# One-hot operands laid out contiguously, and a root product issued in pieces, in a graph network kernel

## The chip, the cores and the metric

The kernel runs on one NeuronCore of a Trainium2 chip. The metric is the device time of one execution in microseconds (us). The engines are TensorE (PE; its weight loads are listed as PEld), VectorE (DVE), ScalarE (ACT), GpSimd (POOL) and SyncE (SP, which here issues DMAs).

## The reference

A stack of graph convolutions over 625 nodes with 768 features and 10625 edges. The first layer is relational, with 34 edge types:

```python
h = relu(layernorm(x))                       # 625 x 768
seg = edge_type * n + dst                    # 34 * 625 segments
agg = segment_sum(h[src], seg)
cnt = segment_sum(ones, seg)
mean = agg / maximum(cnt, 1)
h1 = einsum('rni,rio->no', mean, W_rel) + h @ W_root + b_rgcn
...                                          # then four GCN and three RGCN layers, 3 edge types
```

The edges (src, dst, edge_type) are inputs and are known only on the device, so the kernel sorts them there.

## The kernel before

**Preparation** (`prepare`, the first 248 us) sorts the edges by type into *slots*: 186 tiles of 128 slots, three tiles to a *unit*, each unit of one edge type. Sorting is done with one-hot matrices and matmuls. The edges lie as 125 partitions x 85 columns.

- *Ranks.* VectorE makes `is_key` (edge type one-hot), TensorE sums it per column (`ps_tile`), over partitions (`lower`) and over columns (`offsets`, `bases`), into six PSUM banks. VectorE multiplies and adds these up to one position for each edge (`place`), and from it `slot_of` and `tile_of`.
- *Slots.* In five chunks of 17 columns VectorE makes `is_slot` (17 x 128), `is_tile` (17 x 186) and two products `at_slot` (source and destination number in the slot). For each column TensorE runs two matmuls (`slots(n)`): weights `at_slot[:, n % 2, i, :, c]`, streamed operand `is_tile[:, n % 2, :, c]`. The column number `c` is the innermost dimension of both, so one column's elements are 17 elements (34 bytes) apart. One chunk is 34 matmuls. Buffers are double: chunk n waits for `chunk_used` of n-2.
- *Counts.* `is_node` (128 slots x 125 nodes, six groups of 31 tiles) are the weights of 186 matmuls with five streamed columns (`counts(n)`), which give the number of edges of each node in each unit.
- *Inversion.* After ranks of the nodes within a unit, ten steps (`is_rank_of(i)` on VectorE, `invert(i)` with 31 matmuls on TensorE; 128 weight columns, 31 elements apart, nine streamed columns) give each unit's list of target nodes, `row_list`.
- *Root product.* `h @ W_root + b` in fp32, ten outputs of 125 x 384 (`root(n)`), each a bias matmul and six matmuls. The profile counts each of these fp32 matmuls twice (x12 for six). The ten calls stand at chosen places between the steps above. ScalarE copies each out (`take(n)`), and SyncE stores two of them at a time to DRAM (`sums`), as 125 rows.

Then all engines meet at a barrier.

**Means** (`add_means`, 248 to 998 us) loops over about 34 units: gather 384 rows, select and sum them with `pick` matmuls, multiply with the unit's 768 x 768 weights (loaded each unit, fp32 split in two parts), scatter-add to `sums`. `pick` is made from `slot_dst` and the unit's target list `list_now`, read back from the DRAM tensor `targets`. *Beside* the units the same sort is done for the later layers with their 3 edge types: units 0 to 3 make places on VectorE; in the next five units VectorE makes `is_tile` (2 x 120 x 17) and `is_slot` (128 x 17) and TensorE runs `columns(n)` behind the unit's products: 17 matmuls of 240 streamed columns, again with `c` innermost. The order of work on every engine is the order of the code. A second pass repeats `columns` once behind the last unit for keys with many edges. The layers follow (998 to 1912 us); nothing in them is touched.

## Time and profile before

| | |
|---|---|
| time, three runs | median 1918.2 us (1913.0 to 1918.44) |
| the profiled execution | 1914.25 us, its span 1912.6 us |
| PE busy, PEld busy | 1792.1 us (94%), 1594.5 us (83%) |
| DVE, ACT, POOL busy | 956.0 (50%), 632.5 (33%), 314.7 (16%) |
| granted TensorE clock, mean | 0.928 |

Busy time is the time in which an engine has an instruction in work; a busy TensorE need not run at its peak. The span is from the first to the last instruction of the profiled execution; its own time is 1.65 us more. A granted clock of 1.00 is 2.4 GHz, and 0.50 is 1.2 GHz.

### The profile page before, as it was taken

How to read it: one execution, taken by the hardware profiler on the slowest of the kernel's cores; microseconds unless marked ns; L12 is line 12 of the kernel's file. 1: busy time of each engine (PE TensorE's matmuls, PEld its weight loads, DVE VectorE, ACT ScalarE, POOL GpSimd, SP SyncE). 2: the span in 40 equal slices, each digit the busy share in tenths (PEclk: the TensorE clock that was granted, in tenths of full speed). 3: DMA queues.
4: the chain of work that ended last, by engine and by line, in shares of the span. 5: the costliest groups of instructions: out<-in, count | busy, mean ns of one | idle time of the engine just before them, and what ended most of it. 6: DMA issues, size and time to landing. Idle time of an engine off the chain costs nothing. (4 is left out here: it accounts for less than half of the span.)

```text
span 1912.6 us, 28877 instructions
## 1 busy us (share of the span) xinstructions
PE 1792.1 (94%) x10081; PEld 1594.5 (83%) x10082; DVE 956.0 (50%) x1439; ACT 632.5 (33%) x853; POOL 314.7 (16%) x277
## 2 busy tenths in 40 slices
PE   5999969999999999999958897999999999899988
PEld 2458668777899999898848897999988999899988
DVE  6313559756667766765445556223333333433363
ACT  3200045534555555565422223122112222222220
POOL 0000036353334444444220000000000000000000
PEclk9765789999999999999978998999998999999999
DMA  3210058655879878998533121222112222132111
GB/s 119 93 36 0 19 168 227 187 160 162 231 201 266 233 213 238 267 283 248 152 67 107 58 64 45 55 69 84 39 33 75 75 74 63 34 96 59 38 50 48
DMA packets 96001, 226.47 MB, mean 118 GB/s; under 512 B 10274, under 2 KB 36116, under 8 KB 95940
## 3 DMA queue, kind: packets, MB, share of 16 engines
q1 hardware_dynamic: 72951, 153.22, 25.4%
q0 software_dynamic: 19104, 70.00, 15.8%
q10 hardware_dynamic: 3885, 2.41, 0.4%
q8 instruction: 42, 0.69, 0.2%
q14 instruction: 19, 0.16, 0.0%
HBM read 186.23 MB, written 39.36 MB: 118 GB/s over the span
## 5 line engine op out<-in xcount | busy, mean ns | idle before, releaser
L521 PE MATMUL layers_ps_o<-layers_w_hi,layers_g_hi 128*125 128x384 f32 (+1 forms) x1040 | 360.8, 347 | 4.2 <-DVE layers_w_lo L387 4.2
L522 PE MATMUL layers_ps_o<-layers_w_lo,layers_g_hi 128*125 128x384 f32 (+1 forms) x1040 | 360.4, 347 | 0.0
L523 PE MATMUL layers_ps_o<-layers_w_hi,layers_g_lo 128*125 128x384 f32 (+1 forms) x1040 | 359.9, 346 | 0.0
L1955 PE MATMUL l_means_ps<-l_means_w_hi,l_means_g_hi 128*128 128x512 f32 (+1 forms) x912 | 239.6, 344 | 7.1 <-DVE l_means_g_lo L1813 7.1
L1955 PE MATMUL l_means_ps<-l_means_w_hi,l_means_g_lo 128*128 128x512 f32 (+1 forms) x912 | 236.4, 340 | 0.0
L1955 PE MATMUL l_means_ps<-l_means_w_lo,l_means_g_hi 128*128 128x512 f32 (+1 forms) x912 | 235.4, 340 | 0.0
L1602 ACT CAST l_means_w_hi<-w_raw 128x768 fp32r<-128x768 f32 x204 | 170.3, 838 | 196.3 <-PE l_means_ps L1955 184.8
L1802 DVE TENSOR_TENSOR l_means_w_lo<-w_raw,l_means_w_hi 128x768 fp32r<-128x768 f32 x204 | 187.0, 949 | 75.4 <-ACT l_means_w_hi L1602 57.9
L548 PE MATMUL layers_ps_g<-a,h_hi 125*128 125x316 f32 x840 | 197.1, 317 | 28.4 <-DVE h_lo L158 12.2
L521 PEld LDWEIGHTS layers_ps_o<-layers_w_hi,layers_g_hi 128*125 128x125 f32 x1040 | 193.8, 186 | 11.2 <-issue 5.9
L523 PEld LDWEIGHTS layers_ps_o<-layers_w_hi,layers_g_lo 128*125 128x125 f32 x1040 | 193.7, 186 | 5.3
L522 PEld LDWEIGHTS layers_ps_o<-layers_w_lo,layers_g_hi 128*125 128x125 f32 x1040 | 193.6, 186 | 5.2
L548 PE MATMUL layers_ps_g<-a,h_lo 125*128 125x316 f32 x840 | 196.1, 316 | 0.0
L1939 PE MATMUL l_means_ps<-l_means_pick,l_means_e_hi 128*128 128x256 f32 (+1 forms) x612 | 171.6, 309 | 15.9 <-DVE l_means_e_lo L1797 15.2
L1955 PEld LDWEIGHTS l_means_ps<-l_means_w_hi,l_means_g_hi 128*128 128x128 f32 x912 | 153.4, 190 | 26.6 <-DVE l_means_w_lo L1802 4.2
L324 ACT CAST layers_w_hi<-layers_w_raw 128x768 fp32r<-128x768 f32 (+1 forms) x104 | 89.9, 865 | 256.9 <-PE layers_ps_o L523 247.6
L1955 PEld LDWEIGHTS l_means_ps<-l_means_w_lo,l_means_g_hi 128*128 128x128 f32 x912 | 154.7, 190 | 20.8
L1955 PEld LDWEIGHTS l_means_ps<-l_means_w_hi,l_means_g_lo 128*128 128x128 f32 x912 | 154.8, 189 | 19.7
L406 DVE SCALAR_TENSOR_TENSOR h_rows<-layers_ps_o,layers_inv_rows,h_rows 125x768 f32<-125x768 f32 (+1 forms) x45 | 47.8, 1062 | 247.0 <-PE layers_ps_o L523 246.9
L548 PEld LDWEIGHTS layers_ps_g<-a,h_hi 125*128 125x128 f32 x840 | 146.0, 196 | 30.0 <-DVE h_lo L158 12.7
L1939 PE MATMUL l_means_ps<-l_means_pick,l_means_e_lo 128*128 128x256 f32 (+1 forms) x612 | 168.8, 305 | 0.7 <-issue 0.7
L1534 POOL DMA_INDIRECT sums<-l_means_y,l_means_row_now x76 | 130.3, 1714 | 204.5 <-ACT l_means_y L1637 180.9
(305 smaller groups left out, 2234.5 us busy)
## 6 DMA issues: line engine op xcount, KB each, us to landing
w_raw<-in_L_gnn_W_rel SPq DMA_DIRECT2D x204, 384.0 KB, 7.4
layers_w_raw<-in_L_gnn_w_rel SPq DMA_DIRECT2D x39, 384.0 KB, 3.3
layers_w_raw<-in_L_gnn_w_rel SPq DMA_DIRECT2D x21, 448.0 KB, 4.1
layers_a_raw<-adj SPq DMA_DIRECT2D x9, 769.0 KB
layers_w_raw<-in_L_gnn_W SPq DMA_DIRECT2D x18, 384.0 KB, 5.4
l_means_list_now<-targets SPq DMA_DIRECT2D x34, 192.0 KB
layers_w_raw<-in_L_gnn_w_root SPq DMA_DIRECT2D x13, 384.0 KB, 3.9
layers_w_raw<-in_L_gnn_w_root SPq DMA_DIRECT2D x7, 448.0 KB, 6.2
```

Source lines behind the costliest of these rows:

```text
L324: nc.scalar.copy(w_hi[:, f, :], w_raw[:, f % ring, :]).then_inc(w_hi_ready, 1)
L406: v.scalar_tensor_tensor(to, ps, by, base, ALU.mult, ALU.add).then_inc(o_taken, 1)
L521: t.matmul(out, g_hi[:, f, rows], w_hi[:, f, cols], start=(f == 0), stop=False)
L522: t.matmul(out, g_hi[:, f, rows], w_lo[:, f, cols], start=False, stop=False)
L523: mm = t.matmul(out, g_lo[:, f, rows], w_hi[:, f, cols], start=False, stop=(f == fc - 1))
L548: mm = t.matmul(ps_g[:, buf, at:at + PART[p]], rows[:, k, f * 128:(f + 1) * 128], a[:, k, cols], start=(k == 0 and part == 0), stop=(k == ...
L1534: nc.gpsimd.indirect_dma_start(out=sums, in_=y[:, j, :], in_offset=None, compute_op=ALU.add, out_offset=bass.IndirectOffsetOnAxis(ap=row_n ...
L1602: nc.scalar.copy(w_hi[:, f, :], w_raw[:, f, :]).then_inc(w_hi_ready, 1)
L1802: v.tensor_tensor(w_lo[:, f, :], w_raw[:, f, :], w_hi[:, f, :].bitcast(F32), ALU.subtract)\
L1939: mm = t.matmul(sums, e[:, j, f * 128:(f + 1) * 128], pick[:, j, 0:cols], start=(j == 0 and part == 0), stop=(j == UNIT - 1 and part == 1))
L1955: mm = t.matmul(ps_y[j][:, o0:o1], g[:, f, at], w[:, f, o0:o1], start=(f == 0 and opens and g is g_hi and w is w_hi), stop=(f == fc - 1 an ...
```

## The change

1. The one-hot operands of `slots` and `columns` have the slot or tile number innermost and the column outside. VectorE's comparisons take their second operand in short repeated runs (`SLOT_RUN` 8, `TILE_RUN` 6, `KEY_RUN` 5): `slot_of`, `tile_of`, `loads_by`, `values` and `tile_sums` are stored 5 to 8 times over. The expanded counters `slot_iota` and `tile_iota`, which ScalarE made, are gone.
2. `is_node` has 128 columns for each tile in place of 125.
3. The root product goes in pieces of one matmul (60 in all): four behind each chunk of slots, one behind each group of counts, ten behind the turned counts, one behind each of eight inversion steps, the rest at the end. The bias is split in two fp32r rows.
4. The statistics and scales of the layer norm stand before the places on VectorE, and the transposes of `h` before the first slots on TensorE. The sum that gives `lots` goes ahead of the rank matmuls.
5. Each half of a root tile is stored alone, as 112 and 13 rows.
6. The first unit's target list is made by a matmul on the chip (`ps_first`); the lists are stored to `targets` in the next block.

```diff
-        at_slot = slot_flat[0:EP].rearrange("p (b i s c) -> p b i s c", b=2, i=2, c=chunk)
-        is_tile = tile_flat[0:EP].rearrange("p (b t c) -> p b t c", b=2, c=chunk)
+        at_slot = slot_flat[0:EP].rearrange("p (b i c s) -> p b i c s", b=2, i=2, c=chunk)
+        is_tile = tile_flat[0:EP].rearrange("p (b c t) -> p b c t", b=2, c=chunk)
...
-                then(v.tensor_tensor(is_slot[:], slot_iota[:], slot_of[:, at].unsqueeze(1).broadcast_to([EP, SLOT, chunk]),
-                                     ALU.is_equal))
+                then(v.tensor_tensor(in_runs(is_slot[:], SLOT_RUN),
+                                     by_runs(iota[0:EP, 0:SLOT], SLOT_RUN).unsqueeze(1).broadcast_to(slot_rows),
+                                     slot_of[:, at].unsqueeze(2).broadcast_to(slot_rows), ALU.is_equal))
...
-                                node_of[:, n * group:(n + 1) * group].unsqueeze(1).broadcast_to([SLOT, NP, group]),
+                                node_of[:, n * group:(n + 1) * group].unsqueeze(1).broadcast_to([SLOT, SLOT, group]),
...
-                t.matmul(out, ones_f[:, 0:NP], bias_row[:, cols], start=True, stop=False)
-                for f in range(fc):
+            def root(count):
+                for i in range(done[0], done[0] + count):
+                    n, f = i // fc, i % fc
...
+                        t.matmul(out, one_row[:, 0:NP], bias_hi[:, cols], start=True, stop=False)
+                        t.matmul(out, one_row[:, 0:NP], bias_lo[:, cols], start=False, stop=False)
                     mm = t.matmul(out, root_g[:, f, n // 2 * NP:(n // 2 + 1) * NP], root_w[:, f, cols],
                                   start=False, stop=(f == fc - 1))
...
-                        mm = t.matmul(ps_slot[:, i, 0:tiles], at_slot[:, n % 2, i, :, c], is_tile[:, n % 2, :, c],
+                        mm = t.matmul(ps_slot[:, i, 0:tiles], at_slot[:, n % 2, i, c, :], is_tile[:, n % 2, c, :],
...
+            for n in range(EC // chunk):
+                slots(n)
+                root(4)
+            for n in range(tiles // group):
+                counts(n)
+                root(1)
...
             for i in range(2 * NT):
                 invert(i)
-                if i == 4:
-                    root(7)
+                root(1 if i < 8 else 0)
...
+            t.matmul(ps_first, ones[:], first_list[:].rearrange("p t s -> p (t s)"), start=True, stop=True)\
+                .then_inc(first_spread, 1)
+            root(2)
+            root(10 * fc - done[0])
...
-            for to, count_to, times in ((slot_iota, SLOT, COLUMNS), (tile_iota, tiles2, COLUMNS), (node_iotas, NP, LOTS)):
...
-                    mm = t.matmul(ps_b[:, 0:2 * tiles2], is_slot[:, :, c], is_tile[:, :, :, c],
+                    mm = t.matmul(ps_b[:, 0:2 * tiles2], is_slot[:, c, :], is_tile[:, c, :, :],
```

On TensorE between the first slots and the third chunk, before (`prep_ps<-prep_is_tile,prep_at_slot` are the slots, `prep_root_w,prep_root_g` the root product, `h_rows` the transposes):

```order
L1139 MATMUL prep_ps<-ident,h_rows 128x125 x4
L1160 MATMUL prep_ps<-prep_is_tile,prep_at_slot 128x186 [waits prep_chunk_ready]
L1160 MATMUL prep_ps<-prep_is_tile,prep_at_slot 128x186 x33
L1150 MATMUL prep_ps<-prep_bias_row,prep_ones_f 125x384 [waits prep_root_g_ready,prep_root_loaded]
L1152 MATMUL prep_ps<-prep_root_w,prep_root_g 125x384 x6
L1160 MATMUL prep_ps<-prep_is_tile,prep_at_slot 128x186 [waits prep_chunk_ready]
L1160 MATMUL prep_ps<-prep_is_tile,prep_at_slot 128x186 x33
L1150 MATMUL prep_ps<-prep_bias_row,prep_ones_f 125x384
L1152 MATMUL prep_ps<-prep_root_w,prep_root_g 125x384 x6
L1150 MATMUL prep_ps<-prep_bias_row,prep_ones_f 125x384 [waits prep_o_taken]
L1152 MATMUL prep_ps<-prep_root_w,prep_root_g 125x384 x6
```

and now:

```order
L1178 MATMUL prep_ps<-ident,h_rows 128x125 x4
L1209 MATMUL prep_ps<-prep_is_tile,prep_at_slot 128x186 [waits prep_chunk_ready]
L1209 MATMUL prep_ps<-prep_is_tile,prep_at_slot 128x186 x33
L1197 MATMUL prep_ps<-prep_bias_hi,prep_one_row 125x384 [waits prep_one_row_ready,prep_root_g_ready,prep_bias_ready,prep_root_loaded]
L1198 MATMUL prep_ps<-prep_bias_lo,prep_one_row 125x384
L1199 MATMUL prep_ps<-prep_root_w,prep_root_g 125x384 x4
L1209 MATMUL prep_ps<-prep_is_tile,prep_at_slot 128x186 [waits prep_chunk_ready]
L1209 MATMUL prep_ps<-prep_is_tile,prep_at_slot 128x186 x33
L1199 MATMUL prep_ps<-prep_root_w,prep_root_g 125x384 x2
L1197 MATMUL prep_ps<-prep_bias_hi,prep_one_row 125x384
L1198 MATMUL prep_ps<-prep_bias_lo,prep_one_row 125x384
L1199 MATMUL prep_ps<-prep_root_w,prep_root_g 125x384 x2
```

The transposes of `h_rows` moved ahead of all slots; the root product's two whole outputs and more became four matmuls behind each chunk.

On TensorE behind the last slots, before (rows of 128 x 5 and 125 x 5 are the counts):

```order
L1160 MATMUL prep_ps<-prep_is_tile,prep_at_slot 128x186 x33
L1170 MATMUL prep_ps<-prep_is_tile,prep_at_slot 125x5 [waits prep_nodes_ready]
L1170 MATMUL prep_ps<-prep_is_tile,prep_at_slot 125x5 x30
L1170 MATMUL prep_ps<-prep_is_tile,prep_at_slot 125x5 [waits prep_nodes_ready]
L1170 MATMUL prep_ps<-prep_is_tile,prep_at_slot 125x5 x30
L1150 MATMUL prep_ps<-prep_bias_row,prep_ones_f 125x384 [waits prep_o_taken]
L1152 MATMUL prep_ps<-prep_root_w,prep_root_g 125x384 x6
L1170 MATMUL prep_ps<-prep_is_tile,prep_at_slot 125x5 [waits prep_nodes_ready]
L1170 MATMUL prep_ps<-prep_is_tile,prep_at_slot 125x5 x30
```

and now:

```order
L1209 MATMUL prep_ps<-prep_is_tile,prep_at_slot 128x186 x33
L1199 MATMUL prep_ps<-prep_root_w,prep_root_g 125x384 x2
L1197 MATMUL prep_ps<-prep_bias_hi,prep_one_row 125x384 [waits prep_o_taken]
L1198 MATMUL prep_ps<-prep_bias_lo,prep_one_row 125x384
L1199 MATMUL prep_ps<-prep_root_w,prep_root_g 125x384 x2
L1219 MATMUL prep_ps<-prep_is_tile,prep_at_slot 128x5 [waits prep_nodes_ready]
L1219 MATMUL prep_ps<-prep_is_tile,prep_at_slot 128x5 x30
L1199 MATMUL prep_ps<-prep_root_w,prep_root_g 125x384
L1219 MATMUL prep_ps<-prep_is_tile,prep_at_slot 128x5 [waits prep_nodes_ready]
L1219 MATMUL prep_ps<-prep_is_tile,prep_at_slot 128x5 x30
L1199 MATMUL prep_ps<-prep_root_w,prep_root_g 125x384
```

The counts have 128 rows of output, and a root matmul stands behind each group of 31.

On VectorE from the tile numbers on, before (L1005 to L1010 are the first chunk's one-hots, L88 the statistics; the places are made ahead of these rows):

```order
L997 CAST prep_tile_of<-prep_tile_i 125x85 [waits prep_step]
L1005 TENSOR_TENSOR prep_is_slot<-prep_slot_iota,prep_slot_of 125x2176 [waits prep_iotas_ready,prep_step]
L1007 TENSOR_TENSOR prep_is_tile<-prep_tile_iota,prep_tile_of 125x3162 [waits prep_step]
L1010 TENSOR_TENSOR prep_at_slot<-prep_is_slot,prep_loads 125x2176 x2
L1013 ISA [waits prep_step]
L1017 TENSOR_SCALAR prep_type_row<-prep_ps 62x62 [waits prep_types_summed]
L1018 TENSOR_SCALAR prep_type_col<-prep_ps 62x1 [waits prep_step]
L1019 CAST s_plan<-prep_type_row 1x62 [waits prep_step]
L1020 TENSOR_SCALAR prep_same_type<-prep_type_row,prep_type_col 62x62
L88 BN_STATS prep_stats<-x_rows 125x6 [waits prep_x_loaded1]
L88 BN_STATS prep_stats<-x_rows 125x6
```

and now, behind the statistics and ahead of the tile numbers (L1015 makes the places):

```order
L97 BN_AGGR prep_moments<-prep_stats 125x2 x4
L99 TENSOR_SCALAR prep_var<-prep_moments 125x5 [waits prep_step]
L100 RECIPROCAL prep_rstd<-prep_var 125x5 [waits prep_step]
L78 TENSOR_TENSOR prep_tmp<-prep_rstd 125x5 [waits prep_rooted]
L79 TENSOR_TENSOR prep_tmp<-prep_tmp,prep_var 125x5 [waits prep_step]
L80 TENSOR_SCALAR prep_tmp<-prep_tmp 125x5 [waits prep_step]
L81 TENSOR_TENSOR prep_rstd<-prep_rstd,prep_tmp 125x5 [waits prep_step]
L1003 SCALAR_TENSOR_TENSOR prep_shift<-prep_moments,prep_rstd 125x5 [waits prep_step]
L1005 TENSOR_TENSOR prep_bias_lo<-prep_at_slot,prep_bias_hi 1x768 [waits prep_bias_hi_ready]
L1015 TENSOR_TENSOR prep_early<-prep_ps,prep_early 125x1530 [waits prep_ranked]
L1015 TENSOR_TENSOR prep_early<-prep_ps,prep_early 125x1020 [waits prep_ranked,prep_step]
L1015 TENSOR_TENSOR prep_early<-prep_ps,prep_early 125x340 [waits prep_ranked,prep_step]
```

The scales and the low part of the bias, and the statistics ahead of them, moved from behind the first chunk to before the places.

## Rows read from the trace of the kernel before

**Rows 1.** Windows view: busy time, granted clock (PEclk), DMA share by stage.
```profile
core 0: us, PE busy (x) PEld busy (x) DVE busy (x) ACT busy (x) POOL busy (x), PEclk, DMA share, GB/s
35.00:127.00 92.00, 91.56 (x256) 42.28 (x256) 29.41 (x41) 19.86 (x32) 0.00 (x0) 0.75 0.17 55
127.00:180.00 53.00, 48.37 (x202) 44.03 (x200) 15.54 (x16) 0.48 (x1) 4.10 (x3) 0.56 0.08 23
180.00:247.00 67.00, 56.52 (x404) 38.15 (x404) 34.66 (x46) 3.24 (x8) 0.00 (x0) 0.73 0.06 19
247.00:975.00 728.00, 710.81 (x4166) 622.32 (x4167) 483.70 (x812) 379.34 (x540) 303.26 (x247) 0.96 0.76 214
```

**Rows 2.** Timeline, TensorE: start, duration, op, shape, count; slots, then root products.
```profile
71.53 11.65 PE L1160 MATMUL prep_ps<-prep_is_tile,prep_at_slot 125*128 125x186 f16 x34
...
84.67 6.97 PE L1152 MATMUL prep_ps<-prep_root_w,prep_root_g 128*125 128x384 f32 x12
...
92.41 4.13 PE L1152 MATMUL prep_ps<-prep_root_w,prep_root_g 128*125 128x384 f32 x12
```

**Rows 3.** Timeline, VectorE, one-hots of a chunk; idle before and its releaser in brackets.
```profile
83.21 1.36 DVE L1005 TENSOR_TENSOR prep_is_slot<-prep_slot_iota,prep_slot_of 125x2176 f16<-125x2176 f16 x1 [13.61 <-PE prep_ps L1160]
84.61 1.90 DVE L1007 TENSOR_TENSOR prep_is_tile<-prep_tile_iota,prep_tile_of 125x3162 f16<-125x3162 f16 x1
...
127.54 0.35 DVE L1030 TENSOR_SCALAR s_src_index<-prep_ps 128x186 int32<-128x186 f32 x1 [38.49 <-PE prep_ps L1160]
```

**Rows 4.** Timeline, VectorE, the start of the program.
```profile
17.98 0.15 DVE L969 COPY prep_ends<-prep_ps 34x1 f32<-34x1 f32 x1 [5.05 <-PE prep_ps L1201]
...
20.94 3.56 DVE L986 TENSOR_TENSOR prep_early<-prep_ps,prep_early 125x1530 f32<-125x1530 f32 x3 [0.93 <-PE prep_ps L1205]
24.53 4.05 DVE L991 TENSOR_TENSOR prep_early<-prep_early 125x1445 f32<-125x1445 f32 x6
...
35.96 3.76 DVE L88 BATCH_NORM_STATS2 prep_stats<-x_rows 125x6 f32<-125x384 f32 x8
```

**Rows 5.** Timeline, TensorE and VectorE, counts and inversion.
```profile
153.49 26.82 PE L1170 MATMUL prep_ps<-prep_is_tile,prep_at_slot 128*125 128x5 f16 x124
...
180.35 0.48 DVE L1049 TENSOR_SCALAR prep_present<-prep_ps 125x310 f16<-125x310 f32 x1 [11.19 <-PE prep_ps L1170]
...
197.42 3.85 PE L1179 MATMUL prep_ps<-prep_tile_iota,prep_early 125*128 125x9 f16 x62
...
217.53 6.75 DVE L1064 TENSOR_TENSOR prep_early<-prep_early,prep_rank_lo 125x3968 f16<-125x3968 f16 x3 [6.91 <-PE prep_ps L1179]
```

**Rows 6.** Timeline, the means loop and its second pass: VectorE, SyncE, TensorE.
```profile
374.42 0.56 DVE L1813 TENSOR_TENSOR l_means_g_lo<-l_means_ps,l_means_g_hi 128x384 fp32r<-128x384 f32 x1 [9.13 <-ACT l_means_g_hi L1616]
...
465.04 0.34 SPq L1477 DMA_DIRECT2D l_means_list_now<-targets  x1
...
491.29 0.34 SPq L1477 DMA_DIRECT2D l_means_list_now<-targets  x1
...
509.36 0.34 SPq L1477 DMA_DIRECT2D l_means_list_now<-targets  x1
...
979.23 7.56 PE L1903 MATMUL l_means_ps<-e_raw,l_means_again_slot 125*128 125x240 f16 x17 [3.63 <-DVE e_raw L1768]
```

**Rows 7.** Timeline and source line L1911, TensorE: contiguous f16 columns (ns min/median/max).
```profile
496.94 0.71 PE L1911 MATMUL l_means_ps<-l_means_is_dst,l_means_is_src 128*125 128x315 f16 x4
...
L1911 PE MATMUL l_means_ps<-l_means_is_dst,l_means_is_src x124: 295/298/507, 496.9 to 992.4; 128*125 128x315 f16 x124
```

**Rows 8.** Timeline, VectorE, one-hots in runs of four.
```profile
990.16 0.42 DVE L1782 TENSOR_TENSOR l_means_is_src<-l_means_node_iotas,l_means_slot_src 128x500 f16<-128x500 f16 x1 [2.83 <-issue]
```

**Rows 9.** Timeline, three waits: fifth unit, last store, first selection.
```profile
350.35 1.01 PE L1955 MATMUL l_means_ps<-l_means_w_hi,l_means_g_hi 128*128 128x512 f32 x2 [2.88 <-DVE l_means_g_lo L1813]
...
240.99 0.26 SPq L833 DMA_DIRECT2D sums<-h_rows  x1
...
251.84 1.08 DVE L1791 TENSOR_SCALAR l_means_pick<-l_means_list_now,s_slot_dst 128x384 fp32r<-128x384 f32 x3 [20.55 <-DMA l_means_list_now<-targets]
```

More of the change, by code:

```diff
@@ L976, in _ @@
             v.tensor_scalar(behind[:], iota[0:types, 0:units], ends[:, 0:1], None, ALU.is_ge).then_inc(behind_ready, 1)
+            for k in range(1, NT):
+                ins = statistics(k)
+            then(ins)
+            row_scales(v, then, dve, inverted, rooted, 1, moments, stats, var, rstd, tmp, range(NT))
+            v.scalar_tensor_tensor(shift[:], moments[:, :, 0], -1.0, rstd[:], ALU.mult, ALU.mult).then_inc(scales_ready, 1)
+            dve.wait_ge(bias_hi_ready, 1)
+            v.tensor_tensor(bias_lo[:], bias_raw, bias_hi[:].bitcast(F32), ALU.subtract).then_inc(bias_ready, 1)
             for b0, b1 in ((0, 3), (3, rank_banks - 1), (rank_banks - 1, rank_banks)):
@@ L1188, in _ @@
             mm.then_inc(tiles_summed, 1)
+            pe.wait_ge(sums_copied, 1)
+            t.matmul(ps_total, tile_sums[:, :, 0], ones[0:EC, 0:2], start=True, stop=True, skip_group_check=True)\
+                .then_inc(totalled, 1)
             for b in range(rank_banks):
@@ L1202, in _ @@
                 .then_inc(lots_summed, 1)
+            pe.wait_ge(offsets_ready, 1)
+            for b in range(rank_banks):
+                t.matmul(ranks(b), ones[0:EC, 0:EP], offsets[:, keys_of(b), :].rearrange("p k c -> p (k c)"),
+                         start=False, stop=False, skip_group_check=True)
             pe.wait_ge(bases_ready, 1)
@@ L1210, in _ @@
                 .then_inc(types_summed, 1)
-            slots(0)
+            pe.wait_ge(placed, 1)
             for f in range(fc):
                 turn(f)
-            slots(1)
-            root(0)
-            slots(2)
-            root(1)
-            root(2)
-            slots(3)
-            root(3)
-            slots(4)
-            counts(0)
-            counts(1)
-            root(4)
-            for n in range(2, tiles // group):
+            for n in range(EC // chunk):
+                slots(n)
+                root(4)
+            for n in range(tiles // group):
                 counts(n)
+                root(1)
             pe.wait_ge(present_ready, 1)
@@ L1277, with add_means @@
 Background = namedtuple("Background", "src dst etype kinds adj adj_all ident h node_types emb")
-def add_means(nc, tag, units, w_rel, rows, sums, plan, src_index, slot_dst, row_index, row_inv, targets, e_raw, w_raw, second):
+def add_means(nc, tag, units, w_rel, rows, sums, plan, src_index, slot_dst, row_index, row_inv, targets, list_rows, list_now,
+              e_raw, w_raw, second):
     width = rows.shape[1]
```

252 lines of the change are left out of this document (142 added, 110 removed).

## The prediction

> **What bounds the kernel now.** I read the windows by stage first. From 35 to 247 us TensorE is busy for nearly all of the time, but its granted clock is 0.75, 0.56 and 0.73, against 0.96 in the means loop, and VectorE is busy for less than half [rows 1]. So preparation is bound by a TensorE that is slow, not short of work. The timeline says what at. A chunk of slots is 34 matmuls of 186 f16 columns in 11.65 us, 343 ns each or 1.84 ns a column [rows 2]. The 315 contiguous f16 columns of L1911 come four in 0.71 us with the last one's 0.30 us in it, so one each 137 ns, 0.43 ns a column [rows 7]. The slots stream elements 34 bytes apart, and VectorE waits for them: 13.6 us before a chunk, 38.5 us before `src_index` [rows 3]. The counts take 26.82 us for 124 matmuls of five columns, 216 ns each; the inversion's, with nine columns, take 3.85 us for 62, 62 ns each [rows 5]. Their weights lie 62 bytes apart alike; 125 columns against 128 is what differs. The means loop is TensorE's too (710.8 of 728 us busy), and the `columns` blocks in it are the slots again: 17 in 7.56 us (the second pass's row; five more of this shape stand in the loop), 445 ns for 240 columns, 1.85 ns a column [rows 1, 6].
>
> **The change part by part.** All against the profiled execution, 1914.25 us.
>
> *Start of chunk 0, later by 3 us.* VectorE's places end at 28.6 us (24.53 + 4.05). Of the waits before them (5.05 and 0.93 us for TensorE, whose strided `offsets` go contiguous and whose `lots` go ahead) I leave 0.5: -5.5. Ahead come the statistics, 3.76 us, some twelve small operations at 0.15 to 0.2, 2.2, and `bias_lo`, 0.95 (768 elements; the adds do 2805 in 4.05 us) [rows 4]. With 0.3 for the runs of five (below) the places end at 30.3. The wider `slot_of` and `tile_of` and the type rows make 2.3, a chunk's one-hots 5.6: ready at 38.1. ScalarE's new copies (`loads_by`, `bias_hi`) stand behind three that it has anyway and end well before; if not, each us late is a us lost.
>
> *One-hots in short runs.* The 2176-element and 3162-element operations take 1.36 and 1.90 us in runs of 17 [rows 3]. Nine cycles of 0.96 GHz for each run of 17 give 1.20 and 1.74, and leave 0.16 us fixed for both; the 500 elements in runs of four take 0.42, which is 0.26 + 0.16 [rows 8]. So runs of 8 and 6 should go at two elements a cycle: 1.29, 1.80, 1.29, 1.29, a chunk 5.6 us. Bound above: one a cycle, 10.7 us. The Trainium skill (Vector Engine (DVE) Microarchitecture Reference, 5.1 Performance modes) says that with two sources a pair may span two rows of odd length, so that odd runs would waste nothing. The rows differ: without the half-filled cycle the fixed parts would be 0.23 and 0.25, and 0.42 for the 500 would be too short. By the page the `offsets` in runs of five (2890 elements) would cost 1.66 us, by the rows 1.97, the 0.3 above; the sum by the page would be 0.3 us less.
>
> *Slots, 127.54 to 68.9.* A matmul of 186 contiguous columns is 81 ns at full clock by 0.43 ns a column (62 ns, the inversion's, bounds it below), 34 are 2.75 us; at half clock 5.5. A root piece is two of the profile's matmuls: 0.69 us at clock 1 (4.13 / 12), 1.16 in the stretch at about half (6.97 / 12) [rows 2]. Bias matmuls appear nowhere in this type; a pair for every six pieces I price as a piece. So slots and four pieces make 6.0 us at full clock and 10.9 at half, against VectorE's 5.6. I take the first at 10, as TensorE comes from idling, and the others at 6.0 (dense, as in the means loop): 38.1 + 10 + 18 + 2.75 = 68.9. **-58.6**.
>
> *Counts, 52.8 to 21.7.* To the first group stays at 4.6 (`is_node` costs 0.05 more); the four pieces behind the last slots lie beside it. Then six steps of 31 x 66 ns = 2.05 and a piece of 0.69 to 1.16, together 2.95, above `is_node`'s 2.3; the last piece is not waited for, 0.3 for handshakes: 4.6 + 17.7 - 0.9 + 0.3. From `src_index` to `present` it is 52.8 us now [rows 3, 5]. **-31.1**.
>
> *From `present` to the last store's issue, 60.6 now* [rows 5, 9]. 34 pieces remain where 30 stood, but seven bias pairs' cheap matmuls replace five fp32 ones, and pieces go between inversion steps where TensorE waits for 2.25 us of `is_rank` [rows 5]. TensorE is busy for 56.5 of 67 us [rows 1], so little is to be had. **0**, from -5 to +4.6 (four pieces at half clock).
>
> *Last store.* One of 375 KB in 125 rows is issued at 240.99 and the block ends near 247; halves of 112 and 13 rows spread otherwise. **-2.5**, from 0 to -3.5.
>
> *First selection.* `pick` waits for a DMA that was issued at the block's start [rows 9]; the list is on the chip now, and ScalarE's `e_hi` is late next. **-2.9**, from 0 to -3.3.
>
> *Columns in five units.* A unit with a block takes 26.25 us (465.04 to 491.29), the next without one 18.07 [rows 6]: 8.2, of which the block itself is 7.56, the rest a slower clock behind it. 17 x 104 ns = 1.8 remain. VectorE's operations lie beside products; it idles 9.13 us at a time there [rows 6], and if this cover went, they would cost 5.2 us a unit. **-32**, from -18 (new block at half clock, slow tail stays) to -33.
>
> *Expanded counters gone from ScalarE.* TensorE waits 2.88 us behind them before the fifth unit [rows 9]; wider `slot_of` and `tile_of` on VectorE give 1 back. **-2**.
>
> *Second pass.* Its block stands alone, from idle: 17 x 0.2 = 3.5 in place of 7.56, and 1.2 more on VectorE ahead. **-3**.
>
> Sum: 58.6 + 31.1 + 2.5 + 2.9 + 32 + 2 + 3 = 132.1, so 1782 for the profiled execution. The median of the runs shown, 1918.2, lies 4 us above it, and runs differ by 5; I say **1784**.
>
> **The rivals.**
> - *TensorE stays at half clock in preparation.* For it: the clock there is 0.56 to 0.75 now [rows 1], weight-bound counts and inversion remain between the pieces, and 84.67 shows seven us of root work that did not lift it [rows 2]. Against it: the root product at 92.41 ran at 1.0. Slots then end at 38.1 + 4 x 10.9 + 5.5 = 87.2, +18; counts +2, the rest +7: 1811. The Trainium skill (TensorE: Matmul & The Clock Gate, HAM oscillation) ties a lasting full clock to bursts without idle gaps; by that the new order, whose gaps are short, would be the forecast's.
> - *One-hots at one element a cycle.* A chunk takes 10.7 us on VectorE; slots end at 32.5 + 53.5 + 2.9 = 88.9, +20; the second pass +4; the loop covers its share: 1808. Against: the runs of four [rows 8].
> - *Contiguous columns stream no faster* (1.84 ns is then something else): chunks end at 38.1 + 4 x (11.65 + 5.4) + 11.65 = 118, 49 us of the slots' gain gone, and all of the 32 and 3: 1868. Against: 0.43 ns [rows 7].
> - *128 node columns load no faster than 125*: six steps of 7.8 us, 29 us lost: 1813.
> - *Slower than before: the short runs cost far more on VectorE.* With p ns an element, chunks alone take 48.5p + 3 us; beyond 1.65 ns the loop's units stretch too (8.3p each, five), and the second pass by 8.3p. That adds 98p - 104 us, and eats the 132 from p = 2.4; at 2.5 it is 1925. The trace's slowest vector row is near 1.4 (4.05 us for 2805 elements).
>
> **How the numbers follow.** Forecast 0.70; half clock 0.12; one element a cycle 0.07; no gain from contiguity 0.05; none from 128 columns 0.04; slower 0.02. The forecast's own range is 1768 to 1802: below, full clock from the first chunk (-4), steps of 2.75 (-1), -5 between `present` and the store, -1 each elsewhere; above, the bounds of its terms but not all at once. The two next cases at 1808 and 1811 are taken in: **1768 to 1815**. A difference of 0.3% (6 us) is about what can be told here. Faster 0.97, same 0.01, slower 0.02.
>
> **What the changed profile would show.** L1209, slots: 34 in 2.8 to 5.5 us; L1219, counts: 31 in about 2.1; L1041 to L1048: 1.29 and 1.80 us; `src_index` near 69, `present` near 91, the last store's issue near 151; units with `columns` 2 us longer than those without; granted clock above 0.9 from 50 to 90 us. The forecast is wrong if the clock falls between pieces, if VectorE's operations are longer than 1.4 us, or if the loop's units turn to another engine or to DMA once the block is short.

## The result and the profile after

The changed kernel takes **1786.0 us** (median of 4 runs, 1783.4 to 1787.1) beside 1915.6 for the kernel before on the same chip (1911.8 to 1918.4): a ratio of **0.932, 95% interval 0.930 to 0.935**. The profiled execution took 1786.46 us, its span is 1784.8 against 1912.6, so 127.8 us are to be accounted for.

The windows view by the stages of [rows 1]; the slots are two rows here, the counts' row is followed by one of four microseconds in it, the last row is the means loop and most of its second pass:

```profile
core 0: us, PE busy (x) PEld busy (x) DVE busy (x) ACT busy (x) POOL busy (x), PEclk, DMA share, GB/s
38.00:50.00 12.00, 12.00 (x82) 9.54 (x82) 11.85 (x9) 3.41 (x1) 0.00 (x0) 0.84 0.19 76
50.00:69.00 19.00, 19.00 (x136) 13.98 (x136) 12.51 (x19) 5.78 (x9) 1.70 (x2) 1.00 0.09 23
69.00:90.00 21.00, 19.67 (x196) 14.66 (x195) 13.23 (x6) 1.21 (x4) 2.45 (x2) 0.59 0.23 74
78.00:82.00 4.00, 4.00 (x48) 3.21 (x47) 2.92 (x2) 0.00 (x0) 0.00 (x0) 0.50 0.00 0
90.00:150.00 60.00, 58.24 (x421) 39.70 (x420) 36.11 (x50) 3.24 (x8) 0.00 (x0) 0.69 0.06 17
154.00:850.00 696.00, 676.80 (x4169) 611.78 (x4169) 486.87 (x813) 377.15 (x540) 293.00 (x247) 0.99 0.79 223
```

Slots have the full clock from 42 us on (1.00 is 2.4 GHz); counts and most of the inversion do not, though TensorE is busy in nearly all of their time.

TensorE's timeline, slots and counts, which answers to [rows 2, 5]:

```profile
37.93 4.82 PE L1209 MATMUL prep_ps<-prep_is_tile,prep_at_slot 125*128 125x186 f16 x34 [5.63 <-DVEq L1051]
...
43.21 2.85 PE L1199 MATMUL prep_ps<-prep_root_w,prep_root_g 128*125 128x384 f32 x8
45.90 2.91 PE L1209 MATMUL prep_ps<-prep_is_tile,prep_at_slot 125*128 125x186 f16 x34
...
70.99 2.04 PE L1219 MATMUL prep_ps<-prep_is_tile,prep_at_slot 128*128 128x5 f16 x31 [1.33 <-DVE prep_at_slot L1075]
72.89 1.62 PE L1199 MATMUL prep_ps<-prep_root_w,prep_root_g 128*125 128x384 f32 x2
74.30 2.00 PE L1219 MATMUL prep_ps<-prep_is_tile,prep_at_slot 128*128 128x5 f16 x31
76.16 1.62 PE L1199 MATMUL prep_ps<-prep_root_w,prep_root_g 128*125 128x384 f32 x2
```

VectorE's timeline, a chunk's one-hots and the ends of slots and counts, which answers to [rows 3, 5]:

```profile
37.86 1.29 DVE L1041 TENSOR_TENSOR prep_is_slot<-prep_iota,prep_slot_of 125x2176 f16<-125x2176 f16 x1
39.18 1.81 DVE L1044 TENSOR_TENSOR prep_is_tile<-prep_iota,prep_tile_of 125x3162 f16<-125x3162 f16 x1
40.91 2.48 DVE L1048 TENSOR_TENSOR prep_at_slot<-prep_is_slot,prep_loads_by 125x2176 f16<-125x2176 f16 x2
...
66.35 0.35 DVE L1062 TENSOR_SCALAR s_src_index<-prep_ps 128x186 int32<-128x186 f32 x1 [5.88 <-PE prep_ps L1209]
...
90.52 0.48 DVE L1081 TENSOR_SCALAR prep_present<-prep_ps 125x310 f16<-125x310 f32 x1 [5.31 <-PE prep_ps L1219]
```

34 slot matmuls take 2.91 us instead of 11.65. A count group takes its 2 us, but the piece behind it lasts from 72.89 to 74.30, 1.42 us, where at the full clock one takes 0.69 (4.13 for twelve of the profile's matmuls, which is six pieces). So each of the counts' and most of the inversion's steps is 3.28 us, and VectorE's 2.29 us of one-hots is not what they go by.

TensorE's timeline at the end of the fifth `columns` block, where the program leaves the loop of five units, closes the lists (L1973) and enters the next loop:

```profile
349.40 1.92 PE L1960 MATMUL l_means_ps<-l_means_cnt 125*128 125x240 f16 x17
...
351.15 0.17 PE L1973 MATMUL l_means_ps<-l_means_zeros 128*128 128x2 f16 x1
355.63 0.38 PE L1996 MATMUL l_means_ps<-l_means_pick,l_means_e_hi 128*128 128x256 f32 x1 [4.31 <-issue]
```

and SyncE's marks of the units around it, which answer to the three of [rows 6]:

```profile
339.54 0.34 SPq L1522 DMA_DIRECT2D list_now<-targets  x1
...
364.32 0.34 SPq L1522 DMA_DIRECT2D list_now<-targets  x1
...
382.38 0.34 SPq L1522 DMA_DIRECT2D list_now<-targets  x1
```

The blocks are down from 7.56 to 1.92 us, yet the last unit with one is 24.78 us long, only 1.5 shorter than before: behind its block TensorE does nothing for 4.31 us, and the releaser is "issue", which means that the profile shows no semaphore that it waited for.

| From and to | forecast | measured |
| --- | --- | --- |
| start to `src_index` | -58.6 | 127.54 to 66.35: -61.2 |
| `src_index` to `present` | -31.1 | 52.81 to 24.17: -28.6 |
| `present` to the last store's issue | 0 | 60.64 to 60.5: -0.1 |
| last store to the means block's first work on ScalarE | -2.5 | 6.75 to 3.1: -3.7 |
| from there to the means' first matmul | -2.9 | 7.92 to 4.98: -2.9 |
| loop: columns and expanded counters | -34 | -30.4 |
| rest of the means and second pass | -3 | -3.9 |
| layers, from their first matmul | 0 | +3.0 |
| sum, us | -132.1 | -127.8 |

The loop's figure is from the first matmul of the means (255.66 and 159.09) to the first unit without a block (509.36 and 382.38). The layers' first matmul is at 1005.07 and 874.24. What the layers' 3 us are is asked of `after_again`.

The first row of the table holds more than the new layout. Before, from 35.33 to 127.5 us, TensorE spent 57.9 us on slot matmuls, 29.0 on four outputs of the root product between them and 5.3 on the transposes of `h`; now, from 37.93 to 66.35, it is 15.8 and 12.4 us (16 pieces and three bias pairs), and the transposes lie in a wait ahead of the first chunk. So the slot matmuls are 42 of the 61.2 us, the root product 17, of which a part is only moved behind the slots, and the transposes 5; the start is 2.6 later. These shares are read from the rows; no run tries the order of the root product by itself.

### The profile page after: what moved, and what is told of

It is laid out like the page before. It is cut to its first block, busy times and chain, and to the rows that moved or that the text cites. A ratio compares the mean times of both kernels' runs of the same rounds, so it can differ in the third digit from the quotient of the medians.

```text
span 1784.8 us, 28899 instructions
## 1 busy us (share of the span) xinstructions
PE 1672.6 (94%) x10082; PEld 1546.7 (87%) x10083; DVE 960.0 (54%) x1444; ACT 626.4 (35%) x852; POOL 303.4 (17%) x276
## 4 chain that ended last, share of the span: by engine, by line
PE 46%; DVE 3%; DMA 1%; ACT 1%; SPq 0%; issue 0%; DVEq 0%
PE layers_ps_g L548 14%; PE layers_ps_o L521 11%; PE layers_ps_o L522 11%; PE layers_ps_o L523 11%; DVE layers_w_lo L387 1%; DMA layers_w_raw<-in_L_gnn_w_root 1%; DMA layers_w_raw<-in_L_gnn_W_gcn 1%; DVE layers_g_lo L392 1%; PE layers_ps_g L572 0%; SPq L127 0%; ACT layers_w_hi L324 0%; DVE h_rows L406 0%; DVE h_lo L456 0%; DVE layers_stats L88 0%; DVE x_rows L406 0%
## 5 line engine op out<-in xcount | busy, mean ns | idle before, releaser
L1996 PE MATMUL l_means_ps<-l_means_pick,l_means_e_hi 128*128 128x256 f32 (+1 forms) x612 | 165.9, 302 | 14.0 <-DVE l_means_e_lo L1854 9.0
L1996 PE MATMUL l_means_ps<-l_means_pick,l_means_e_lo 128*128 128x256 f32 (+1 forms) x612 | 164.7, 299 | 1.9 <-issue 1.9
```

The costliest lines, as they stand in the source:

```text
L1996: mm = t.matmul(sums, e[:, j, f * 128:(f + 1) * 128], pick[:, j, 0:cols], start=(j == 0 and part == 0), stop=(j == UNIT - 1 and part == 1))
```

## The experiments

Theory A: TensorE's price in the slots and columns was the jump of 34 bytes between streamed elements, in the counts the 125 weight columns; what was not gained lies in pieces that ran at 1.2 GHz and in one idle stretch, in which TensorE's program waited for its own next instructions. The rivals: strided weights; the old order's waits; late data behind the columns.

### Which operand's stride it was

```diff
 # tile_strided
-        is_tile = tile_flat[0:EP].rearrange("p (b c t) -> p b c t", b=2, c=chunk)
+        is_tile = tile_flat[0:EP].rearrange("p (b t c) -> p b c t", b=2, c=chunk)
 # weights_strided
-        at_slot = slot_flat[0:EP].rearrange("p (b i c s) -> p b i c s", b=2, i=2, c=chunk)
+        at_slot = slot_flat[0:EP].rearrange("p (b i s c) -> p b i c s", b=2, i=2, c=chunk)
```

> Edit: the changed kernel with only the slots' tile one-hot (the moving operand, 186 columns) laid out as before, element 34 bytes from element; the weights (at_slot) stay contiguous. Theory A (the price of before was the moving operand's stride): the 34 slot matmuls of a chunk take about 11.65 us again instead of 2.91, a chunk some 14.5 instead of 5.75, src_index comes near 110 instead of 66.4 and the time near 1830 us. Rival B (it was the weights' stride): 34 in about 2.9 us and a time within 8 us of the changed kernel's 1786; what is over comes from VectorE, which now writes with a stride (3162 elements, 1.8 us if that costs nothing, 3.3 if it costs the fast mode).

> Edit: the changed kernel with only the slots' weights (at_slot) laid out as before, 34 bytes from element to element; the moving one-hot stays contiguous. Theory A (only the moving operand's stride costs): 34 slot matmuls in about 2.9 us, weight loads near 0.10 us each; VectorE writes two of its four operations of a chunk with a stride, so a chunk lasts 5.75 us if that is free and 7.9 if they fall to one element a cycle, and the time is 1786 to 1797. Rival B (strided weights cost TensorE): 34 matmuls well above 4 us, up to 11.65, and a time up to 1830.

One run each: 1847.7 and 1862.7 us. The timelines of the first chunks, TensorE and VectorE, of `tile_strided`:

```profile
49.53 11.49 PE L1209 MATMUL prep_ps<-prep_is_tile,prep_at_slot 125*128 125x186 f16 x34 [17.33 <-DVEq L1051]
...
66.81 11.50 PE L1209 MATMUL prep_ps<-prep_is_tile,prep_at_slot 125*128 125x186 f16 x34 [0.46 <-DVEq L1051]
...
50.78 13.60 DVE L1044 TENSOR_TENSOR prep_is_tile<-prep_iota,prep_tile_of 125x3162 f16<-125x3162 f16 x1
```

and of `weights_strided`:

```profile
53.94 5.49 PE L1209 MATMUL prep_ps<-prep_is_tile,prep_at_slot 125*128 125x186 f16 x34 [22.30 <-DVEq L1051]
...
56.91 9.42 DVE L1048 TENSOR_TENSOR prep_at_slot<-prep_is_slot,prep_loads_by 125x2176 f16<-125x2176 f16 x1
```

For TensorE theory A holds: with the moving operand alone strided the chunk is back at 11.5 us (338 ns a matmul), with the weights alone 5.49 at a granted clock of 0.50, 161 ns a matmul. The changed kernel's first chunk takes 4.82, but windows of one microsecond show its granted clock at 0.50 only until 42; less nine matmuls of 81 ns at the full clock, the other 25 take 4.0 us, 160 ns each. In a later chunk, where the granted clock is 1.00 from 100.7 us on, the matmuls with strided weights start some 80 ns apart, as the contiguous ones do. The weights' stride costs TensorE nothing that can be seen at either level. With the moving operand strided, the chunk at a granted clock of 0.50 took 11.49 us and the next, at 0.73, took 11.50: this price does not follow the clock. Both expectations missed VectorE. It writes the strided operand at **4.3 ns an element** (13.6 us for 3162, 9.42 for 2176) where contiguous writes cost 0.57 to 0.59, so both kernels go by VectorE, and their times price that and not TensorE. The Trainium skill (SBUF — State Buffer, Door 1: The DMA port swizzle) tells of lines of 16 bytes, and that accesses which fall in a new line each time pay a penalty; rows of both engines agree that there is one, some 7 times on VectorE and 4 on TensorE at the full clock, and the page gives no size for it. That those lines are the cause here is not shown: no run tries a jump shorter than 16 bytes.

The same jump with four-byte alignment:

```diff
 # tile_stride36
-        tile_flat = sb("is_tile", [SLOT, 2 * tiles * chunk], F16)
+        tile_flat = sb("is_tile", [SLOT, 2 * tiles * (chunk + 1)], F16)
-        is_tile = tile_flat[0:EP].rearrange("p (b c t) -> p b c t", b=2, c=chunk)
+        is_tile = tile_flat[0:EP].rearrange("p (b t c) -> p b c t", b=2, c=chunk + 1)[:, :, 0:chunk, :]
```

> Edit: tile_strided once more, with 36 bytes from element to element of the moving one-hot instead of 34. Theory A (any jump between elements costs, whether or not it is a multiple of four bytes): 34 slot matmuls near 11.5 us, VectorE's write of 3162 elements near 13.5 us (4.3 ns each), about 1848 us. Rival B (34 bytes are dear since elements lie across four-byte words in turn): at 36 bytes both prices fall to half or less, 34 matmuls near 6 us and the write near 6.8.

1850.7 us in one run: 34 matmuls in 11.49 us again, VectorE's write 13.7 us on average. It is the jump, not its alignment to four bytes.

### Runs of an odd length

```diff
 # tile_run3
-TILE_RUN = 6
+TILE_RUN = 3
```

> Edit: the changed kernel with the slots' tile numbers held in runs of three instead of six, so that VectorE's operation on 3162 elements reads runs of three. Theory A (a run of an odd length is rounded up to the next even one at two elements a cycle): 3162 x 4/3 elements, about 2.36 us instead of 1.81, a chunk of VectorE 6.2 us instead of 5.7, the slots up to 2.5 us longer, 1786 to 1789. Rival B (pairs run on over the ends of runs): 1.81 us and 1786.

1788.8 us in one run. VectorE's groups by line and shape in the stretch of the slots:

```profile
L1044 DVE TENSOR_TENSOR prep_is_tile<-prep_iota,prep_tile_of 125x3162 f16<-125x3162 f16 x5 | 11.8, 2356 | 0.2
L1041 DVE TENSOR_TENSOR prep_is_slot<-prep_iota,prep_slot_of 125x2176 f16<-125x2176 f16 x5 | 6.4, 1286 | 0.2
```

2.356 us, as theory A has it to the last digit that it gave: 0.55 us more for 1054 runs, 0.52 ns for each, which is what one more contiguous element costs (1.81 less 1.29 us, for 986 elements, is 0.53 ns each). A run of three costs as much as a run of four. The rule of the Trainium skill that the prediction set against the rows (Vector Engine (DVE) Microarchitecture Reference, 5.1 Performance modes), pairs that span rows of odd length, would give 1.81; here, where one of the two sources is repeated by a step of 0, the measurement decides against it.

### 125 or 128 weight columns

```diff
 # nodes125: the count one-hots (iota, one-hot, its two buffers, the output's rows)
-s.copy(node_iota, iota[:, 1:SLOT + 1].unsqueeze(2).broadcast_to([SLOT, SLOT, group]))
+s.copy(node_iota, iota[:, 1:NP + 1].unsqueeze(2).broadcast_to([SLOT, NP, group]))
```

> Edit: the changed kernel with 125 node columns instead of 128 in the count one-hots, nothing else. Theory A (a weight load of 125 columns costs the 216 ns of the old pitch, one of 128 some 60 ns): 31 count matmuls in about 6.7 us instead of 2.0, each of six steps 4.8 us longer, the time 27 to 29 us longer: 1814. Rival B (the old pitch came from something else of the old order, such as the buffers it waited for): steps stay 3.3 us, time 1786.

1813.0 us (4 runs, 1811.8 to 1815.9), ratio to before 0.947 (0.945 to 0.949): 27 us slower than the changed kernel. Its counts on TensorE's timeline:

```profile
78.54 6.70 PE L1219 MATMUL prep_ps<-prep_is_tile,prep_at_slot 128*125 128x5 f16 x31
85.09 1.62 PE L1199 MATMUL prep_ps<-prep_root_w,prep_root_g 128*125 128x384 f32 x2
86.51 6.70 PE L1219 MATMUL prep_ps<-prep_is_tile,prep_at_slot 128*125 128x5 f16 x31
```

216 ns a matmul, the pitch of [rows 5], against 60; three columns more make 156 ns less. The pitch is set by the number of weight columns alone. It agrees with the Trainium skill (TensorE: Matmul & The Clock Gate, Weight-path perf modes), where a faster weight load is taken at exactly 128 weights of a type other than fp32; its "~2×" is smaller than the 3.6 here.

### The columns' moving operand, and what the long block hid

```diff
 # columns_strided
-                    tiles[0:EP, 0:2 * tiles2 * COLUMNS].rearrange("p (c a t) -> p c a t", a=2, c=COLUMNS))
+                    tiles[0:EP, 0:2 * tiles2 * COLUMNS].rearrange("p (a t c) -> p c a t", a=2, c=COLUMNS))
```

> Edit: the changed kernel with only the moving one-hot of the later graph's column steps (is_tile, 240 columns) laid out as before. Theory A: a block of 17 takes 7.56 us again instead of 1.92, five blocks 28 us, the second pass 3 to 4, and TensorE's idle 4.31 us behind the last block is gone, since it was there before too but lay under the long block: the time is 1786 + 28 + 3 - 4 to 6 = 1811 to 1813. Rival B (the idle time comes from something else, a transfer or the one-hots): it stays at about 4.3 us, and the time is 1817 or more.

1934.2 us (4 runs), ratio **1.010 (1.008 to 1.012)**: 1.0% slower than the kernel before, clear of the noise though small. Theory A's time was 121 us off (B had said only 1817 or more), since three of VectorE's four operations write with the stride, 8.8 us each, and TensorE waits for them. Its timeline at the last block:

```profile
472.35 7.47 PE L1960 MATMUL l_means_ps<-l_means_cnt 125*128 125x240 f16 x17 [20.02 <-DVE l_means_cnt L1825]
479.65 0.18 PE L1973 MATMUL l_means_ps<-l_means_zeros 128*128 128x2 f16 x1
479.70 0.56 PE L1996 MATMUL l_means_ps<-l_means_pick,l_means_e_hi 128*128 128x256 f32 x1
```

The time says nothing on the question asked. The rows say that the block is at 7.47 again and that the idle stretch behind it is gone, as A had it; since TensorE waits 20 us ahead of the block, late data would have had time to arrive too, so this run alone does not decide against B. This run also shows the outcome of the rival that the prediction put at 0.02, by another cause: with VectorE at 4.3 ns an element, here through its strided writes and not through short runs, the kernel is slower than before. The contiguous writes of the changed kernel are what keeps it from that.

### The idle stretch

The list of DMA queues by kind, in windows of 0.2 us, shows one packet of the queue of kind "instruction" that starts between 352.8 and 353.0 in the changed kernel and one between 479.0 and 479.2 in the kernel before, whose long block ran until about 482.3:

```profile
q8 instruction: 1, 0.02, 29.5%
```

29.5% of 16 engines for 0.2 us is 0.94 us for its 0.02 MB. TensorE goes on 2.7 us after the packet's start. The idle stretch is a property of this place in the code: it stands there again in `after_again` (4.71 us) and in the six edits that leave this code alone, `tile_strided`, `weights_strided`, `tile_stride36`, `tile_run3`, `nodes125` and `pieces_out` (4.36 to 4.70 us), and each time TensorE goes on 2.7 to 2.9 us after the start of such a packet. Late data are not the reason: what the first matmul behind it reads, `pick`, `e_hi` and `e_lo`, had been made by 342.0 us, over 13 us before. Two edits move code, and one of them adds empty instructions:

```diff
 # split_loop
-            with pe.Fori(0, list_units) as n:
+            with pe.Fori(0, 2) as n:
+                one_unit(unit(n + LEAD))
+                columns(n)
+            with pe.Fori(2, list_units) as n:
 # pad_code, at the start of TensorE's program for the means (pad is a new semaphore)
+            for _ in range(128):
+                t.nop().then_inc(pad, 1)
```

> Edit: the changed kernel with TensorE's loop of five units and column blocks written as two loops, of two and of three passes, the same instructions in the same order. Theory A (the 4.31 us of idle time behind the last block come from leaving a loop for code that has not been read yet, with only 1.92 us of work queued ahead of it): a second idle stretch of 3 to 5 us appears behind the second block, and the time grows by 3 to 6 us, to about 1791. Rival B (it comes from a transfer, from the clock, or from data that are late at that one place): no second idle stretch, 1786.

> Edit: the changed kernel with 128 empty instructions at the start of TensorE's program for the means, where the engine waits some 9 us anyway, so that all code behind them lies 128 instructions further on. Theory A (the idle 4.31 us behind the last column block are TensorE's program waiting for its next block of instructions, which a packet of the instruction queue brings; where it falls is set by where the code lies): the idle stretch is gone from that place or clearly shorter, and another may show at another place; 1780 to 1788 us. Rival B (it belongs to that place, through the loop's end or late data): it stays there at 3.5 to 5 us, 1786.

`split_loop`: 1786.6 us (5 runs, 1784.1 to 1793.5), ratio 0.932 (0.930 to 0.934). The place of its idle time:

```profile
295.32 1.92 PE L1960 MATMUL l_means_ps<-l_means_cnt 125*128 125x240 f16 x17
300.53 0.38 PE L1996 MATMUL l_means_ps<-l_means_pick,l_means_e_hi 128*128 128x256 f32 x1 [3.30 <-issue]
...
358.31 0.17 PE L1973 MATMUL l_means_ps<-l_means_zeros 128*128 128x2 f16 x1
358.34 0.36 PE L1996 MATMUL l_means_ps<-l_means_pick,l_means_e_hi 128*128 128x256 f32 x1
```

The stretch did not double, as A had it; it moved. Behind the second block, where the new loop's code begins, TensorE idles 3.30 us (an instruction packet starts between 297.6 and 297.8), and behind the last block, where it had idled 4.31, it goes straight on. A later stretch of 3.17 us stands at 660, behind a packet at 657.7. `pad_code`: 1805.8 us (5 runs), ratio 0.943 (0.942 to 0.945). The empty instructions were not hidden: TensorE's wait ahead of the means is 25.50 us instead of 8.97, and its first matmul stands at 175.31 instead of 159.09; its time is therefore not evidence. Its rows are:

```profile
368.49 0.17 PE L1974 MATMUL l_means_ps<-l_means_zeros 128*128 128x2 f16 x1
...
373.60 0.28 PE L1997 MATMUL l_means_ps<-l_means_pick,l_means_e_hi 128*128 128x256 f32 x1 [1.97 <-issue]
...
671.99 0.58 PE L1997 MATMUL l_means_ps<-l_means_pick,l_means_e_hi 128*128 128x256 f32 x1 [5.94 <-issue]
```

The stretch behind the last block is gone too: TensorE goes straight on and stops some way into the next unit, for 1.97 us, and for 5.94 at a place where the changed kernel did not idle. Packets start at 371.2 and 669.2, 2.4 and 2.8 us before TensorE goes on. In every trace, then, the idle stretch has an instruction packet just ahead of TensorE's going on, no semaphore that it waits for, and a place that moves with the code: what is late is code. The profile does not say for which engine a packet is, so this rests on times and places. That it belongs to every loop's end, as my theory first had it, fell; where it falls is set by where the code lies, and whether it costs by how much work is queued ahead. What sets the packets' places and lengths is open.

The remedy is to end the loop on long work:

```diff
 # columns_inside
             with pe.Fori(0, list_units) as n:
-                one_unit(unit(n + LEAD))
-                columns(n)
+                one_unit(unit(n + LEAD), beside=lambda: columns(n))
 # in the products of a unit
                     for f in range(fc):
+                        if f == fc - 1 and beside is not None:
+                            beside()
```

> Edit: the changed kernel with TensorE's column block ahead of the last sixth of the unit's products instead of behind them, so that the loop ends on some twelve to eighteen 0.35 us matmuls. Theory A (leaving the loop is what costs, and only short work covers it): the idle 4.31 us fall under 1.5 and the time by 3 to 5 us, to about 1782. Rival B (late data at that place): the idle time stays near 4.3 us, 1786. Rival C: the one-hots, which VectorE ends only 0.7 us before the new place, are late in the other units, up to 1 us each: 1787 to 1791.

1778.0 us (5 runs, 1777.5 to 1780.5), ratio 0.928 (0.926 to 0.930), against 1785.9 (1782.9 to 1787.3) for the changed kernel run beside it: 7.9 us, more than A's 3 to 5. TensorE's timeline at the same end of the loop:

```profile
347.99 1.92 PE L1960 MATMUL l_means_ps<-l_means_cnt 125*128 125x240 f16 x17
...
351.87 0.18 PE L1973 MATMUL l_means_ps<-l_means_zeros 128*128 128x2 f16 x1
351.90 0.36 PE L1996 MATMUL l_means_ps<-l_means_pick,l_means_e_hi 128*128 128x256 f32 x1
```

No idle time at this place, no late one-hots, though a packet starts here too (at 354.1): there is work queued ahead of it. A part comes back earlier: ahead of the first unit with a block, at 248 us, TensorE idles 2.64 us on "issue", where the changed kernel idles 1.07. The two units at this place are 18.8 and 18.1 us apart by SyncE's marks (340.28, 359.10, 377.16) instead of 24.8 and 18.1, which is 6.0 of the gain: 4.3 idle, the rest the slower clock after it (from 356 to 358 us the granted clock is 0.50 in the changed kernel and 1.00 here). From the means' first matmul to the layers' first it is 709.3 us, against 715.2 and 717.9 in the changed kernel's two profiles, and the layers add up to 3.7 us of difference between executions; the 1.9 us that are left of the 7.9 are within that.

### The pieces

```diff
 # pieces_out
                 counts(n)
-                root(1)
...
-            root(10)
+            root(8)
...
                 invert(i)
-                root(1 if i < 8 else 0)
 # ScalarE: the turned counts are copied after take(3) instead of after take(5)
```

> Edit: the changed kernel without the root product's pieces behind the six count steps and eight of the ten inversion steps; eight and six pieces stand behind the ranks and the whole counts, the other 26 at the end, and ScalarE copies the turned counts before it takes two of the root's results, so that it needs fewer pieces done by then. Theory A (a piece costs 1.42 us of the way in these steps, where the granted clock is 1.2 GHz, and 0.69 at the end at 2.4 GHz; the steps then go by VectorE, 2.35 us): present at about 84.6 instead of 90.5, the inversion over at about 121 instead of 139.5, the root's end at about 142 instead of 150: the time falls by 6 to 8 us, to about 1779. Rival B (the clock stays at 1.2 GHz for the pieces at the end too): 26 pieces take 37 us instead of 18 and the time grows by about 10 us, to 1796.

1780.1 us (5 runs, 1779.7 to 1782.1), ratio 0.929 (0.927 to 0.931): 5.8 us less than the changed kernel, A's 6 to 8 nearly. Steps on TensorE's timeline, in the counts and at the end:

```profile
73.45 2.04 PE L1219 MATMUL prep_ps<-prep_is_tile,prep_at_slot 128*128 128x5 f16 x31 [0.17 <-DVE prep_at_slot L1075]
75.67 2.01 PE L1219 MATMUL prep_ps<-prep_is_tile,prep_at_slot 128*128 128x5 f16 x31 [0.18 <-DVE prep_at_slot L1075]
...
126.75 6.32 PE L1199 MATMUL prep_ps<-prep_root_w,prep_root_g 128*125 128x384 f32 x12
...
142.75 4.13 PE L1199 MATMUL prep_ps<-prep_root_w,prep_root_g 128*125 128x384 f32 x12
```

Steps are 2.2 us and go by VectorE, `present` comes at 84.37 (forecast 84.6), the inversion ends at 121.7 (121), and the root at 146.9 instead of 142: the granted clock is 0.50 until 131 us, so the first five or so of the last 26 pieces still ran at 1.2 GHz (6.32 us for six, half of them slow, that take 4.13). So a half-clock piece costs 1.42, and moving it behind more pieces gets 0.7 back, but not for all. The first matmul of the means stands 3.2 us earlier; the rest of the 5.8 is in later stages and stays unexplained; it is no more than what two executions of the same code differ by.

### Both, and the changed kernel once more

`both` is the two edits above in one kernel; `after_again` has no edit.

> Edit: columns_inside and pieces_out together. Theory A (the two gains lie in different stages and add): 7.9 us and 5.8 us off 1785.9, that is about 1772 us. Rival B (TensorE's idle stretch comes back at another place, since the code has shifted): up to 4.3 us of it is lost again, 1775 to 1777.

1774.6 us (5 runs, 1772.7 to 1774.8), ratio **0.9265 (0.925 to 0.928)**, the fastest version: 11.4 us below the changed kernel's 1785.9, which was measured on another chip. Its TensorE has two waits on "issue" (0.84 and 2.30 us, the second at 242.0), as `columns_inside` has (0.79 and 2.64), so the second edit brings no further stretch back, and B is not borne out; the sum fell 2.3 us short all the same, and why is open.

> Edit: none; the changed kernel once more, beside the others of this call. Both theories expect a time within 2 us of 1786. Its profile tells whether the 3.2 us by which the layers were longer in the changed kernel's profiled run, in code that the change does not touch, come back (a property of the kernel) or not (a difference between executions).

1785.9 us (5 runs), ratio 0.931 (0.929 to 0.933). The layers, from their first matmul to the end, in windows of before, of the changed kernel and of this run:

```profile
1005.07:1912.60 907.53, 861.90 (x4975) 837.73 (x4975) 362.96 (x477) 208.77 (x259) 0.00 (x0) 0.96 0.21 61
```

```profile
874.24:1784.80 910.56, 866.56 (x4975) 842.38 (x4975) 362.76 (x477) 208.55 (x259) 0.00 (x0) 0.96 0.21 61
```

```profile
877.34:1785.60 908.26, 862.83 (x4975) 838.35 (x4975) 362.77 (x477) 208.48 (x259) 0.00 (x0) 0.97 0.21 61
```

Here 0.7 us more than before, 3.0 in the first profile. With 906.5 in `pieces_out` and 911.0 in `split_loop`, the same code differs by 4.5 us between executions; the layers are no part of the change.

## Why the prediction was right, point by point

1784 was said and 1786.0 measured, in the likeliest case's own range. The mechanisms that carry the sum (contiguous columns, 128 weight columns, one-hots in short runs) were right. That the total came within 2 us is in part luck: the slots gave 2.6 us more than forecast and the counts 2.5 less, the loop 3.6 less, the layers 3.0 less through nothing but a difference between executions; profile against profile it is 1782 forecast and 1786.46 measured. Its steps:

- **Chunk 0 ready** at 38.1, measured 37.9. **One-hots** at 1.29 and 1.80, measured 1.29 and 1.81; the rule that the prediction drew from the rows, with odd runs rounded up, held, and `tile_run3` confirmed it apart. One reading is wrong beside it: the slowest vector row of the kernel before is not 1.4 ns an element but the scan of 2550 elements (L1698) in 5.46 us, 2.1 ns; no term hangs on it.
- **Slots**: the step "a matmul of 186 contiguous columns is 81 ns" held: a steady chunk's 34 matmuls and the piece behind them start 2.74 us apart (45.90 and 48.64), 81 ns each, and `tile_strided` shows that the moving operand's jump was the whole price of these matmuls. The first chunk with its pieces took 8.0 us instead of 10, since the clock rose behind its matmuls (its pieces ran at 0.69); the others 5.8 instead of 6.0. The term is -61.2, not -58.6.
- **Counts**: "128 against 125" is confirmed by `nodes125`. Mis-sized was the piece between, "0.69 to 1.16": it took 1.42, a step 3.28 instead of 2.95. The 1.16 was read from a stretch in which the clock was only partly low. The term is -28.6, not -31.1. "Granted clock above 0.9 from 50 to 90 us" did not come (0.59 from 69 to 90), and the prediction's own sign, a clock that falls between pieces, was there. The half-clock rival was thus right for counts and inversion: its +2 for the counts came, its +7 for the rest did not, and the +18 for the slots that carried its price did not either. The Trainium skill (TensorE: Matmul & The Clock Gate, HAM oscillation), which the prediction weighed, ties the fall of the clock to idle gaps. Here from 74 to 90 us TensorE is busy without a gap at a granted 0.50, and from 104 to 136, busy without a gap too, the clock goes from 1.00 (until 113) to 0.50 (from 116): the measurement decides against it.
- **From `present` to the last store 0**: held in sum, but not by its reasons. Pieces were to go into the inversion's steps where TensorE waits for VectorE; at 1.42 us they made the steps TensorE's, 3.28 instead of 2.3, and `pieces_out` took 3 us out of the counts and this stage together.
- **Last store and first selection**: -3.7 and -2.9, forecast -2.5 and -2.9; the first lies just outside its bound of -3.5. Neither was tried by itself.
- **Columns**: "a slower clock behind it" goes with the long block, was the thought, for all five. It held for four (each unit with a block is 6.5 to 7.8 us shorter by SyncE's marks, against 6.4 in the forecast); at the fifth an idle stretch of 4.31 us came up that the 7.56 us had hidden. No step of the prediction asked what else the long block hid. The term, with the counters, is -30.4, not -34.
- **Second pass**: -3.9 with the rest of the means against -3; its block takes 3.58 us, forecast 3.5.

## What to carry to other kernels

Lay out what TensorE streams so that its elements are contiguous, but reach that by VectorE operations whose innermost run is short, even and contiguous; changing the view alone moves a larger price (4.3 ns an element) to VectorE. Give TensorE 128 weight columns even where three are waste. When a long block becomes short, ask what it hid: code still on its way, or a low granted clock beside the short matmuls that remain (0.50 here), at which dense work put between them costs double.

## What was unexpected of the hardware

- VectorE writes f16 elements 34 or 36 bytes apart at 4.3 ns each, against 0.57 to 0.59 ns contiguous (13.6 us for 3162; 8.8 for 2040).
- The strided stream costs TensorE 338 ns for 186 columns at granted clocks of 0.50 and 0.73 alike; contiguous ones take 160 ns at 0.50 and 81 at 1.00. Strided weights cost it nothing.
- TensorE at 100% busy, with 31 short matmuls and a piece in turn, is granted 0.50; the short matmuls keep their 60 ns at either level, the pieces take 0.69 or 1.42 us.
- TensorE can stand still for 2 to 6 us with nothing to wait for in the profile while a packet of instructions is brought, and go on 2.4 to 2.9 us after the packet's start; 128 empty instructions, each with a semaphore's increment, took it some 16 us more than the wait that they were to hide in.
